# Attention with group norm on one core: TensorE's waiting places reordered, two more units rounded, their rests on VectorE

## The reference

```
h    = group_norm(x, 8 groups) * gn_w + gn_b
q, k, v = qw h + qb,  kw h + kb,  vw h + vb
attn = softmax(q^T k / sqrt(128))            # 1024 x 1024 for each image
out  = x + pw (v attn^T) + pb
```

## Time and profile before

| | |
|---|---|
| median of 3 runs | 134.87 us (134.65 to 138.57) |
| the profiled execution | 134.62 us, of which its span is 132.9 |
| PE busy | 124.7 us (94% of the span) |
| DVE busy | 98.6 us (74%) |
| ACT busy | 84.9 us (64%) |
| POOL busy | 69.7 us (52%) |
| DMA moved | 21.01 MB, mean 158 GB/s |
| granted clock of PE | 1.0 of full speed over the span |

### The profile page before, as it was taken

The page is one execution under the profiler, slowest core; times in us unless marked ns, Lnnn a source line. Parts: engine busy times, 40 slices in busy tenths (PEclk is TensorE's granted clock), DMA queues, the critical chain, the costliest instruction groups (busy, mean ns, idle before and its releaser), DMA issues.

```text
span 132.9 us, 2364 instructions
## 1 busy us (share of the span) xinstructions
PE 124.7 (94%) x767; PEld 110.2 (83%) x767; DVE 98.6 (74%) x159; ACT 84.9 (64%) x149; POOL 69.7 (52%) x51
## 2 busy tenths in 40 slices
PE   5899999998699999999999999999999999699991
PEld 5897887886587889999898888898888999698991
DVE  0577878999969878989699999756987898130421
ACT  4055588768967996968756999678595369412000
POOL 5044015950006798696656696866749329923000
PEclk9999999999999999999999999999999999999999
DMA  4970000023896398899684898699738896897502
GB/s 129 286 297 0 0 5 0 0 42 81 201 215 138 122 213 205 190 239 213 167 195 125 199 215 185 198 215 222 184 142 197 204 210 221 197 212 165 178 20 99
DMA packets 9712, 21.01 MB, mean 158 GB/s; under 512 B 2378, under 2 KB 4196, under 8 KB 9700
## 3 DMA queue, kind: packets, MB, share of 16 engines
q1 hardware_dynamic: 8960, 20.59, 61.4%
q10 hardware_dynamic: 740, 0.28, 0.8%
HBM read 4.07 MB, written 2.11 MB: 46 GB/s over the span
## 4 chain that ended last, share of the span: by engine, by line
PE 80%; issue 6%; DVE 4%; DMA 3%; ACT 2%; POOL 2%; SPq 0%; POOLq 0%
PE ACC L471 16%; PE S L384 10%; PE S L385 9%; PE S L388 9%; PE ACC L442 6%; PE A L364 5%; PE ACC L444 5%; PE ACC L443 5%; PE S L423 3%; DMA x_sb<-x 3%; PE S L328 2%; POOL p_lo L976 2%; PE ACC L412 2%; DVE s_sb L804 1%; PE ACC L498 1%
## 5 line engine op out<-in xcount | busy, mean ns | idle before, releaser
L804 DVE TENSOR_SCALAR_CACHE_REDUCE s_sb<-S,row_term 128x1024 f32<-128x1024 f32 x32 | 40.9, 1278 | 12.3 <-PE S L388 12.0
L620 ACT ACTIVATE s_sb<-s_sb,rowmin 128x1024 f32<-128x1024 f32 x32 | 36.9, 1154 | 11.1 <-DVE s_sb L804 9.0
L976 POOL TENSOR_TENSOR p_lo<-pT,p_hi 128x1024 fp32r<-128x1024 f32 x14 | 33.4, 2394 | 11.5 <-ACT p_hi L638 11.5
L813 DVE STREAM_TRANSPOSE blocks<-s_sb 128x1024 f32<-128x1024 f32 x28 | 34.7, 1240 | 0.3
L384 PE MATMUL S<-h_hi,g_hi 128*128 128x512 f32 x64 | 27.7, 433 | 0.3 <-issue 0.3
L471 PE MATMUL ACC<-pT,v 128*128 128x128 f32 (+1 forms) x160 | 26.5, 317 | 0.0
L385 PE MATMUL S<-h_lo,g_hi 128*128 128x512 f32 x64 | 25.1, 393 | 0.0
L471 PEld LDWEIGHTS ACC<-pT,v 128*128 128x128 f32 x160 | 23.1, 191 | 2.1
L388 PE MATMUL S<-h_hi,g_lo 128*128 128x512 f32 x64 | 19.8, 391 | 0.0
L442 PE MATMUL ACC<-p_hi,v_hi 128*128 128x256 f32 x56 | 16.4, 293 | 1.2 <-POOL p_lo L976 1.1
L443 PE MATMUL ACC<-p_lo,v_hi 128*128 128x256 f32 x56 | 15.7, 281 | 0.0
(11 more groups left out here) (110 smaller groups left out, 172.5 us busy)
## 6 DMA issues: line engine op xcount, KB each, us to landing
pT<-blocks SPq DMA_DIRECT2D x112, 128.0 KB, 2.4
rden_bc<-row_store SPq DMA_DIRECT2D x6, 256.0 KB, 3.7
x_sb<-x SPq DMA_DIRECT2D x1, 1024.0 KB, 5.9
out<-xb SPq DMA_DIRECT2D x4, 256.0 KB, 3.1
out<-xb SPq DMA_DIRECT2D x7, 128.0 KB, 3.0
x_sb<-x SPq DMA_DIRECT2D x2, 256.0 KB, 3.0
x_sb<-x SPq DMA_DIRECT2D x1, 512.0 KB, 3.8
w_in<-weights ACTq DMA_DIRECT2D x2, 128.0 KB, 3.6
```

The lines of the kernel that those rows point to most:

```text
L620: act.activation(s_sb[:, c % 3, :], s_sb[:, c % 3, :], ACT.Exp, bias=rowmin[:, c % CH:c % CH + 1], scale=-1.0, accum_out=den[:, n % 2, k:k ...
L804: dve.tensor_scalar(s_sb[:, c % 3, :], S[:, c % 2, :], row_term[:, b % 2, i:i + 1], None, ALU.add, ALU.min, accum_out=rowmin[:, i:i + 1]). ...
L813: dve.transpose(blocks_view(n)[:, :, :, k, :].rearrange("p j t q -> p t j q"), s_sb[:, c % 3, :].rearrange("p (t j q) -> p t j q", t=KT, j ...
L976: pool.tensor_tensor(lo, probs, hi.bitcast(F32), ALU.subtract).then_inc(p_lo_ready, 1)
```

## The change

PE's order: the four parts of the first set run in steps 5, 6, 7 and 9 instead of 4, 5, 6 and 9; the deviation matmul of image 2 goes from step 8 to step 9; in image 1, value_tiles(1,0) stands behind the first-set part of step 7, group_vars(2) behind that of step 9, and value_tiles(1,2) behind the value unit of step 10; in the tail the direct unit of chunk 30 goes ahead of unit (6,2). The units (3,1) and (5,1) become rounded ones. Their rests are computed by DVE, behind the reciprocals, and not by POOL. All roundings from set 2 on stand behind the exponentials of step FIRST[n] + u + 6. SP's stores of sets 4 and 5 go behind the move of set 7.

```diff
@@ -19,19 +19,24 @@
...
-FIRST_SET_STEPS = (4, 5, 6, 9)
+FIRST_SET_STEPS = (5, 6, 7, 9)
 FIRST_DIVIDED = 11
...
-DEVIATION_STEPS = (0, 8, 16)
+DEVIATION_STEPS = (0, 9, 16)
 VARIANCE_STEPS = (1, 9, 17)
+CHANNEL_VAR_STEPS = (1, 9, 17)
+
 CHANNEL_STEPS = (6, 7)
-SPLIT_UNITS = ((1, 2), (1, 3), (2, 2), (2, 3), (3, 0), (3, 2), (3, 3), (4, 2), (4, 3), (5, 0), (5, 2), (5, 3), (6, 2), (6, 3))
+SPLIT_UNITS = ((1, 2), (1, 3), (2, 2), (2, 3), (3, 0), (3, 1), (3, 2), (3, 3), (4, 2), (4, 3),
+               (5, 0), (5, 1), (5, 2), (5, 3), (6, 2), (6, 3))
+
+DVE_RESTS = ((3, 1), (5, 1))
@@ -54,11 +59,10 @@
...
-    FIRST_QUARTERS = {FIRST[n] + 7: SPLIT_UNITS.index((n, 0)) for n in (3, 5)}
-    SECOND_QUARTERS = {FIRST[n] + 6 + u: SPLIT_UNITS.index((n, u)) for n in (3, 5) for u in (2, 3)}
-
-    LATER_BATCHES = {FIRST[n] + (8 if n == 6 else 6 + u): [SPLIT_UNITS.index((n, w)) for w in ((2, 3) if n == 6 else (u,))]
-                     for n in (2, 4, 6) for u in (2, 3)}
+    ROUNDS = {}
+    for r, (n, u) in enumerate(SPLIT_UNITS):
+        if n > 1:
+            ROUNDS.setdefault(min(FIRST[n] + u + LAG - 2, STEPS - 2), []).append(r)
     SPREAD_BY_DMA = NS - 2
@@ -187,6 +191,7 @@
...
         v_hi_ready, v_lo_ready, p_hi_ready, p_lo_ready = map(sem, ("v_hi_ready", "v_lo_ready", "p_hi_ready", "p_lo_ready"))
+        p_lo_by_dve = sem("p_lo_by_dve")
         part_done = sem("part_done")
@@ -211,6 +216,10 @@
...
+        def rests(r):
+
+            return sum(unit not in DVE_RESTS for unit in SPLIT_UNITS[:r + 1])
+
         def last_split_unit(b):
@@ -227,7 +236,7 @@
...
             n, u = SPLIT_UNITS[r]
-            return FIRST[n] + u + 1
+            return FIRST[n] + u + (2 if FIRST[n] + u >= STEPS - LAG else 1)
@@ -285,8 +294,10 @@
...
                     spread_rows(n)
-                store_set(n - 2)
-            store_set(LS - 2)
+                if n < LS - 2:
+                    store_set(n - 2)
+            for n in range(LS - 4, LS - 1):
+                store_set(n)
             store_chunk(0)
@@ -416,7 +427,7 @@
...
                 for f in range(HALVES):
-                    pe.wait_ge(pair_ready[f], SETS[0] + SETS[LS])
+                    pe.wait_ge(pair_ready[f], SETS[0] + d + 1)
                 pe.wait_ge(v_ready, VP * B)
@@ -432,7 +443,10 @@
...
                 pe.wait_ge(p_hi_ready, r + 1)
-                pe.wait_ge(p_lo_ready, r + 1)
+                if (n, u) in DVE_RESTS:
+                    pe.wait_ge(p_lo_by_dve, DVE_RESTS.index((n, u)) + 1)
+                else:
+                    pe.wait_ge(p_lo_ready, rests(r))
                 if crosses(n):
@@ -516,23 +530,23 @@
...
                 scores(c)
-                if c == DEVIATION_STEPS[0]:
-                    group_deviations(1)
+                if c in DEVIATION_STEPS[:2]:
+                    group_deviations(DEVIATION_STEPS.index(c) + 1)
                 if late == 0:
...
                     project_g(b, 1)
-                if late == 2:
+                if late == 2 and b != 1:
                     value_tiles(b, 2)
-                if c in DEVIATION_STEPS[1:]:
-                    group_deviations(DEVIATION_STEPS.index(c) + 1)
-                if c in VARIANCE_STEPS:
+                if c == DEVIATION_STEPS[2]:
+                    group_deviations(3)
+                if c in VARIANCE_STEPS and b != 1:
                     group_vars(VARIANCE_STEPS.index(c) + 1)
...
                     project_g(b + 1, 0)
-                if i == 7 and b < L:
+                if i == 7 and 0 < b < L:
                     value_tiles(b + 1, 0)
@@ -540,8 +554,15 @@
...
                     first_set_part(FIRST_SET_STEPS.index(c))
+                if i == 7 and b == 0:
+                    value_tiles(1, 0)
+                if c == VARIANCE_STEPS[1]:
+                    group_vars(2)
                 if c >= LAG + SETS[0]:
                     value_unit(c - LAG)
+                if late == 2 and b == 1:
+                    value_tiles(1, 2)
+            value_unit(DIRECT)
             value_unit(STEPS - LAG)
@@ -550,7 +571,6 @@
...
             value_unit(FIRST[LS - 1] + 1)
-            value_unit(DIRECT)
             value_unit(FIRST[LS - 1] + 2)
@@ -633,7 +653,10 @@
...
                     act.wait_ge(part_done, unit_end(r - 2))
-                    act.wait_ge(p_lo_ready, r - 1)
+                    if SPLIT_UNITS[r - 2] in DVE_RESTS:
+                        act.wait_ge(p_lo_by_dve, DVE_RESTS.index(SPLIT_UNITS[r - 2]) + 1)
+                    else:
+                        act.wait_ge(p_lo_ready, rests(r - 2))
                 probs, hi, lo = split_views(r)
@@ -685,8 +708,6 @@
...
                     copy_v(b, 1)
-                if c in FIRST_QUARTERS:
-                    round_probs(FIRST_QUARTERS[c])
                 if late == 1:
@@ -707,8 +728,6 @@
...
                     copy_pair(c - 1)
-                if c in SECOND_QUARTERS:
-                    round_probs(SECOND_QUARTERS[c])
                 exponentials(c)
@@ -716,8 +735,8 @@
...
                     round_v(ROUND_V_STEPS.index(c))
-                if c in LATER_BATCHES:
-                    for r in LATER_BATCHES[c]:
+                if c in ROUNDS:
+                    for r in ROUNDS[c]:
                         round_probs(r)
@@ -813,6 +832,13 @@
...
+            def split_probs(k):
+                r = SPLIT_UNITS.index(DVE_RESTS[k])
+                dve.wait_ge(p_hi_ready, r + 1)
+                dve.wait_ge(part_done, unit_end(r - 2))
+                probs, hi, lo = split_views(r)
+                dve.tensor_tensor(lo, probs, hi.bitcast(F32), ALU.subtract).then_inc(p_lo_by_dve, 1)
+
             def invert_denominators(n):
@@ -820,7 +846,7 @@
...
             def divide(n):
-                dve.wait_ge(part_done, FIRST[n] + SETS[n])
+                dve.wait_ge(part_done, FIRST[n] + SETS[n] + (1 if n == LS - 2 else 0))
                 if n < SPREAD_BY_DMA:
@@ -834,7 +860,7 @@
...
             def finish_last_chunk(d):
-                dve.wait_ge(part_done, (STEPS - 3, STEPS)[d])
+                dve.wait_ge(part_done, (STEPS - LAG + 1, STEPS)[d])
                 dve.wait_ge(bc_ready, 2)
@@ -845,7 +871,7 @@
...
                 n = LS - 1
-                dve.wait_ge(part_done, FIRST[n] + 2 if part == 0 else STEPS - 1)
+                dve.wait_ge(part_done, FIRST[n] + 3 if part == 0 else STEPS - 1)
                 dve.wait_ge(bc_ready, 1)
@@ -891,8 +917,8 @@
...
                 late = i - 1 if b == 0 else i
-                if c - 1 in DEVIATION_STEPS:
-                    channel_vars(DEVIATION_STEPS.index(c - 1) + 1)
+                if c in CHANNEL_VAR_STEPS:
+                    channel_vars(CHANNEL_VAR_STEPS.index(c) + 1)
                 if c - 1 in VARIANCE_STEPS:
@@ -908,6 +934,9 @@
...
                     invert_denominators(FIRST.index(c) - 1)
+                for k, (n, u) in enumerate(DVE_RESTS):
+                    if c == FIRST[n] + u + LAG - 1:
+                        split_probs(k)
                 if late == 1 and b > 0:
@@ -1009,13 +1038,10 @@
...
                     split_v(ROUND_V_STEPS.index(c - 1))
-                if c - 1 in LATER_BATCHES:
-                    for r in LATER_BATCHES[c - 1]:
-                        split_probs(r)
-                if c in FIRST_QUARTERS:
-                    split_probs(FIRST_QUARTERS[c])
-                if c in SECOND_QUARTERS:
-                    split_probs(SECOND_QUARTERS[c])
+                if c - 1 in ROUNDS:
+                    for r in ROUNDS[c - 1]:
+                        if SPLIT_UNITS[r] not in DVE_RESTS:
+                            split_probs(r)
                 if c == FIRST[1] + LAG:
```

## The result

| | before | changed |
|---|---|---|
| median of 19 runs each | 134.83 us | 135.35 us (134.57 to 139.46) |
| span of the profiled execution | 132.9 | 133.1 |
| PE busy | 124.7 | 124.7 |

The ratio is 1.0032, with a 95% interval of 1.0019 to 1.0044: slower by a third of a percent, which is the case (A) of the prediction. Runs some 4 us above the rest occur in both kernels and are left out of the ratio; in two profiled executions further down (e3 and e8) this is a start of scores 0 that comes 3.9 us later. The profiled execution of the changed kernel began its scores at 11.55 us, the one before at 11.72, so 0.17 is added where a time of one is set against the other.

The account below looks back on a forecast made before the run. PE, busy 124.7 of 132.9 us, was taken to bound the kernel. Terms 0 + 0.36 + 0.25 + 0.73 - 1.34 + 0.2 = +0.2 on 134.62 gave 134.8, with 0.25 to the median 135.1; range 133.3 to 137.4.

Parts of the forecast that it names:

- (A): Whole kernel: the summed terms hold, with DVE's gshift ahead of POOL's rest; 135.1 us, own range 134.5 to 135.9, chance 0.48.
- B: Step 19: gshift loses to POOL's rest, PE waits 2.7 at (3,3); 137.3 us, chance 0.27.
- C: From step 12: DVE, ACT and POOL catch up, rests come in time, PE keeps 2 x 0.31; 133.5 us, chance 0.22.
- Early stage: Steps 4 to 12: PE gains 1.3 us, all waited away for p_lo at (1,2); net 0, bounds -0.4 and +0.3.
- wait for gvar: Step 10: the reciprocals' transpose newly waits for gvar from DVE, at 39.3 instead of 40.61; unit (1,0) from 39.66.
- DVE's rest: Units (3,1), (5,1): takes 1.2 us; at (3,1) PE waits 0.67, less 0.31 saved makes (3,2) 0.36 late.
- (3,3): Set 3: POOL's rest reaches PE at 78.80 against a start at 78.19 before; 0.61 late.
- (5,3): Set 5: its rest arrives at 105.89 against a start at 105.16, +0.73; with set 3's delay, +1.34 together.
- Tail: Direct unit ahead of (6,2): (6,2) 1.78 late, 1.34 given back, (7,2) waits for set 7's data, at 125.0, +0.2.
- deferral of the stores: Tail: set 4's stores no longer ahead of set 7's move bring its data up to 1.3 earlier, only partly counted.
- Race: Step 19: gshift could start at 72.45, POOL's rest at 72.49; DVE first by 0.04 us, less than could be read.
- The sum: All stages against the profiled execution: +0.2, so 134.8, or 135.1 as a median.

Follow-up runs that it names:

- e3: Changed kernel with the rests of (3,1) and (5,1) on POOL instead of DVE; 134.48 us, ratio 0.997.
- e8: Changed kernel, value_tiles(1,2) back ahead of unit (1,0), DVE's rests ahead of transposes, roundings of (3,3), (5,3) ahead of exponentials; 134.95 us, ratio 1.001.
- e2: Changed kernel with value_tiles(1,2) back ahead of the reciprocals' transpose and unit (1,0) in step 10; 133.87 us, ratio 0.9916.
- e7: Changed kernel with SP's stores in the old order, those of set 4 ahead of the move of set 7; 135.08 us, ratio 1.003.
- e6: Changed kernel with a small DVE memset ahead of gshift in step 19; median of 12 times 136.70 us, ratio 1.003 with the longer times left out.
- e5: Kernel before with the reordering of steps 4 to 9, value_tiles(1,2) left in place, and the tail part; 132.67 us, ratio 0.9844.
- e9: e5 with gshift of the last image moved behind drain 18, ahead of transposes 17; 132.36 us, ratio 0.9805.
- e1: Kernel before with the tail part alone: direct unit ahead of (6,2), stores of sets 4 and 5 behind set 7's move; 134.06 us, ratio 0.9945.

## Why the prediction was right

The stated range, 133.3 to 137.4, took in A and most of B and C, so the time alone doesn't tell these apart; the steps do. Step by step, in the clock of the kernel before. Distances of units come from the table.

- **Early stage, net 0.** Expected: PE 1.3 ahead, all of it waited away at (1,2). Measured: 1.26 of waiting, (1,2) at the same place. e2 shows the cause as argued, the place of value_tiles(1,2) in ACT's queue. The new wait for gvar at the reciprocals' transpose was smaller than the 0.35 that follows from my times: gvar started at 38.97 + 0.17 = 39.14, not 39.3, and PE stood for about 0.15. The value tiles came at 41.14 + 0.17 = 41.31, for 41.20 expected, since they began 1.80 behind the start of unit (1,0) and not 1.54. That the two misses nearly cancel is luck. Why it was 1.80 is open.
- **DVE's rest.** 1.2 expected, 1.19 measured; (3,1) 0.67 late expected, 0.70 measured. The unit saved less than 0.31: from (3,1) to (3,2) PE took 75.44 - 72.56 = 2.88 us and not 2.80, so (3,2) was 0.47 late, for 0.36 expected. At (3,3) this no longer counts, as PE waits for POOL's rest there (0.21).
- **(3,3)**: 0.61 expected, 0.59 measured. **(5,3)**: 1.34 expected, 1.30 measured.
- **Tail.** (6,2) 1.78 late expected, 1.81 measured. (7,2): 0.2 expected (0 to 0.77), 0.42 measured (0.35 by its own row, 124.96 + 0.17 - 124.78). This term was 0.2 too small. I had taken 0.55 off for the deferral of the stores; e7 has 0.27, and not even that is shown to come from the deferral, so what it is worth stays open. Without it I had counted 125.55, and e7's row stands at 125.24 + 0.06 = 125.30, so that sum was a little long too.
- **Race.** 0.04 expected between gshift and POOL's rest, 0.05 measured, with DVE first. That it fell this way was partly luck: the prediction itself called 0.04 less than it could read, and gave B 0.27. Three of the 19 times of the changed kernel lie above 138, one of the kernel before; no trace of these was taken, so a lost race in one of them isn't ruled out. e6 shows what the other order costs. The stated price nearly held for the wait (2.24 for 2.15); the clock's fall behind it, 1.5 us more, was in no bound of mine.
- **(C)** had no support: the rests do not catch up, because drain 18 follows its scores at once: it starts at 68.80, and PE's last row of them, from 68.14, is 0.62 long.

The sum was +0.2 on the profiled execution, the measured distance at the last unit is +0.42, and the ratio 1.0032 is 0.43 us.

What the change hides is that two of its parts are good. e5 and e9 keep these and leave the rest.

## What to carry to other kernels

When PE is moved ahead, follow the queues of the engines that PE's moved work feeds, in their own order: a copy that now waits at the head of ACT's queue holds everything behind it, and the gain comes back as a wait some steps later. Before a unit is made cheaper for PE, add up the chain that feeds it and compare with when PE arrives; 0.31 us saved is worth nothing behind a rest that is 0.67 late. And a small DVE instruction that reads two SBUF operands belongs where POOL is idle.

## What the runs showed of the hardware that I had not expected

- How sharp the race between DVE and POOL is. gshift starts 0.05 us ahead of POOL's instruction and takes 0.22 (changed kernel), or 0.22 behind and takes 2.19 (e6). The Trainium skill (SBUF — State Buffer, Who interferes with whom) states just this contention, and that who issues first decides; the traces agree, with 0.22 against 2.19, and with 1.96 against 0.22 in e5 and e9.
- A single wait of 2.43 us of PE was followed by 0.61 of granted clock over the next 4 us (e6), with 0.50, the 1.2 GHz level, from 82 to 85. The waits of up to 1.3 us in the changed kernel left it at 1.0.
- The landing of a moved quarter varies from one execution to the next without any change to the kernel near it. In e1, ACT's rounding of (5,0) started at 93.24, where it had started at 91.82 before, and everything from (5,0) on was 0.6 to 0.7 late:

```profile
93.24 1.05 ACT L640 CAST p_hi<-pT 128x1024 fp32r<-128x1024 f32 x1 [1.51 <-issue]
```

The move of set 5 began 0.38 us later than before (84.60 against 84.22), and its eighth transfer, issued at 89.0 instead of 88.7, took 4.1 us to land instead of 3.1. So it landed at about 93.1 instead of 91.8, just ahead of the rounding in both. Why it took longer is open.
